# Block-diagonal score products of the first layer: one half of the heads for all four token tiles in a call, and the first softmax by half the heads of two tiles

## The reference, cut to what matters

```python
h = einsum('bnd,ade->bane', feat_in, W)
th = tanh(h)
attn = einsum('bane,aeo->bano', th, w_src) + swapaxes(einsum('bane,aeo->bano', th, w_dst), 2, 3)
attn = where(attn >= 0, attn, 0.2 * attn)
attn = softmax(where(~adj, -999.0, attn), axis=-1)
feat_out = einsum('banm,bame->bane', attn, h) + b
out = gate * elu(feat_out) + (1 - gate) * feat_in     # gate = sigmoid(feat_in @ H_w.T + H_b)
```

## Time and profile before

| | us |
|---|---|
| time, median of 3 runs | 1072.71 (1072.68 to 1074.22) |
| the profiled execution's own time | 1072.87 |
| its span from first to last instruction | 1070.8 |
| TensorE busy | 991.1 (93%) |
| VectorE busy | 780.3 (73%) |
| ScalarE busy | 574.5 (54%) |
| GpSimd busy | 277.7 (26%) |

### The profile page before, as it was taken

The page is one execution under the profiler, slowest core; times in us unless marked ns, Lnnn a source line. Parts: engine busy times, 40 slices in busy tenths (PEclk is TensorE's granted clock), DMA queues, the critical chain, the costliest instruction groups (busy, mean ns, idle before and its releaser), DMA issues.

```text
span 1070.8 us, 24885 instructions
## 1 busy us (share of the span) xinstructions
PE 991.1 (93%) x10153; PEld 857.0 (80%) x10153; DVE 780.3 (73%) x1456; ACT 574.5 (54%) x1126; POOL 277.7 (26%) x338
## 2 busy tenths in 40 slices
PE   6589999999999999999999999999999999999686
PEld 5487878888787887978788797878879788887575
DVE  4867867778786777868677886767788676876814
ACT  6556466373746636374564638446463754745331
POOL 2233140502415051240504124050321406032120
PEclk9689999999999999999999999999999999999988
DMA  9211151510414142031413204151241515111102
GB/s 237 32 15 20 29 90 32 90 32 31 61 32 91 31 82 40 31 62 32 91 32 77 41 12 83 31 91 31 65 39 19 91 32 90 32 47 18 28 30 59
DMA packets 183652, 56.41 MB, mean 53 GB/s; under 512 B 164978, under 2 KB 183540, under 8 KB 183540
## 3 DMA queue, kind: packets, MB, share of 16 engines
q1 hardware_dynamic: 183540, 54.83, 28.3%
HBM read 17.06 MB, written 12.58 MB: 28 GB/s over the span
## 4 chain that ended last, share of the span: by engine, by line
PE 55%; DVE 27%; ACT 7%; issue 7%; POOL 0%; ACTq 0%; DVEq 0%; POOLq 0%
PE ps L624 11%; PE ps L610 10%; PE ps L626 10%; PE ps L625 10%; DVE x L948 5%; PE ps L693 5%; PE ps L790 4%; DVE ee L945 4%; ACT p L430 3%; DVE hT1l L1056 3%; DVE hT0l L858 3%; DVE stats L842 3%; DVE p L973 2%; PE ps L808 2%; DVE x_in L996 2%
## 5 line engine op out<-in xcount | busy, mean ns | idle before, releaser
L410 POOL TENSOR_TENSOR x_in<-x_in,ee 128x384 f32<-128x384 f32 x64 | 72.5, 1134 | 626.7 <-DVE ee L951 626.7
L469 ACT ACTIVATE th<-ps 128x384 f32<-128x384 f32 x64 | 31.9, 499 | 209.8 <-DVE v_tok L936 209.8
L1020 DVE TENSOR_TENSOR hT1l<-ps,hT1h 128x512 fp32r<-128x512 f32 x48 | 30.4, 685 | 88.2 <-ACT hT1h L540 88.1
L984 DVE COPY_PREDICATED_SCALAR z<-not_adj,masked 128x768 f32 x64 | 69.4, 1084 | 32.5 <-ACT z L501 32.5
L610 PE MATMUL ps<-ident,p 128*128 128x128 f32 x576 | 76.3, 283 | 17.8 <-ACT p L430 10.0
L403 POOL TENSOR_TENSOR x_in<-x_in,h 128x384 f32<-128x384 f32 x64 | 85.5, 1367 | 18.5 <-DVE Wf_lo L883 18.5
L610 PEld LDWEIGHTS ps<-ident,p 128*128 128x128 f32 x576 | 65.3, 144 | 23.0 <-issue 12.7
L624 PE MATMUL ps<-Wf_hi,hT1h 128*128 128x384 f32 x192 | 69.0, 359 | 10.4 <-DVE hT1l L1056 10.4
L397 POOL TENSOR_TENSOR x_in<-x_in,bf_row 128x384 f32<-128x384 f32 x64 | 62.1, 1003 | 48.0 <-ACT p L430 48.0
L507 ACT ACTIVATE z<-z 128x768 f32<-128x768 f32 x64 | 54.5, 853 | 28.1 <-DVE z L989 28.0
L501 ACT ACTIVATE z<-ps 128x384 f32<-128x384 f32 x128 | 52.5, 497 | 31.0 <-PE ps L693 31.0
(11 more groups left out here) (130 smaller groups left out, 2796.5 us busy)
## 6 DMA issues: line engine op xcount, KB each, us to landing
V<-v_tok SPq DMA_DIRECT2D x128, 192.0 KB, 5.0
x_in<-in_x_dram SPq DMA_DIRECT2D x16, 768.0 KB, 5.0
out_dram<-x_in SPq DMA_DIRECT2D x16, 768.0 KB, 3.6
x<-in_L_gnn_H_w_dram SPq DMA_DIRECT2D x1, 576.0 KB, 5.9
QT<-in_L_gnn_W_dram SPq DMA_DIRECT2D x3, 192.0 KB, 6.7
thT<-in_L_gnn_Wq_dram SPq DMA_DIRECT2D x1, 576.0 KB, 5.8
z<-in_L_gnn_Wk_dram SPq DMA_DIRECT2D x1, 576.0 KB, 6.8
z<-in_L_gnn_Wv_dram SPq DMA_DIRECT2D x1, 576.0 KB, 7.9
```

The source lines that it names most:

```text
L410: pool.tensor_tensor(x_in[:, i % 3, t], x_in[:, i % 3, t], ee[:, t], ALU.subtract).then_inc(x2_made, 1)
L984: dve.copy_predicated(zt, not_adj[:, t].unsqueeze(1).broadcast_to((P, HEADS0, N)), masked0[:].unsqueeze(2).broadcast_to((P, HEADS0, N))).t ...
```

## The change

`blocks` and `leaky` go by halves of the heads instead of pairs of tiles. `blocks(half_of)` takes the banks of all four tiles for one half of the heads. Its eight calls run first over the four tiles of graph 0 of each tile and then over the four tiles of graph 1; the shapes, the number of calls, the operands and the place of both `blocks` in TensorE's program stay. `leaky` goes four times for half 0, then `copy_q(2)`, then four times for half 1. The bank of a job is now that of `4*half_of + t`.

`softmax0` and `exp0` go by a unit: unit 0 is half 0 of tiles 0 and 1, unit 1 half 0 of tiles 2 and 3, units 2 and 3 the same for half 1. A unit has as many elements as a tile had (768 in a partition), but as two runs of 384. `turn_probs` turns in the same order as before; it now waits for the unit in which a block lies, and asks at the middle of a tile as well: 12 waits in 24 turns where there were 8.

```diff
-                def blocks(pair):
-                    take(i, job("leaky_made", 4 * pair + 3))
-                    take(i, job("leaky_made", 4 * pair))
-                    take(i, job("leaky_made", 4 * pair + 1))
-                    take(i, job("leaky_made", 4 * pair + 2))
-                    for half_of in range(2):
-                        for t in (2 * pair, 2 * pair + 1):
+                def blocks(half_of):
+                    for t in range(TILES):
+                        take(i, job("leaky_made", 4 * half_of + t))
+                    for g in range(2):
+                        for t in range(TILES):
                             rows = slice(SD * t, SD * t + SD)
-                            for g in range(2):
-                                mm = pe.matmul(ps[64 * g:64 * g + 64, job("leaky_made", 2 * t + half_of) % BANKS, 0:D],
-                                               src_rows[rows, g * N:(g + 1) * N],
-                                               thT[rows].rearrange("p c m -> p (c m)")[:, (2 * g + half_of) * D:(2 * g + half_of + 1) * D],
-                                               start=True, stop=True, skip_group_check=True)
+                            mm = pe.matmul(ps[64 * g:64 * g + 64, job("leaky_made", 4 * half_of + t) % BANKS, 0:D],
+                                           src_rows[rows, g * N:(g + 1) * N],
+                                           thT[rows].rearrange("p c m -> p (c m)")[:, (2 * g + half_of) * D:(2 * g + half_of + 1) * D],
+                                           start=True, stop=True, skip_group_check=True)
                     mm.then_inc(scores0_full, 1)
...
+                def unit_of(t, pair):
+                    return 2 * (pair // PAIRS1) + t // 2 + 1
...
-                            if k == 0 or pair == 0:
-                                pe.wait_ge(ready, TILES * n + t + 1)
+                            if k == 0 or pair % PAIRS1 == 0:
+                                pe.wait_ge(ready, TILES * n + made(t, pair))
...
-                def softmax0(t):
+                def softmax0(unit):
                     if real(i):
-                        n = TILES * i + t + 1
-                        zt = z[:, t].rearrange("p (h m) -> p h m", m=N)
+                        n = TILES * i + unit + 1
+                        half_of, pair = divmod(unit, 2)
+                        tiles, heads = slice(2 * pair, 2 * pair + 2), slice(PAIRS0 * half_of, PAIRS0 * half_of + PAIRS0)
+                        zu = z[:, tiles, half_of * D:(half_of + 1) * D].rearrange("p t (h m) -> p t h m", m=N)
                         dve.wait_ge(not_adj_made, i + 1)
-                        dve.wait_ge(leaky_made, 8 * i + 2 * t + 2)
+                        dve.wait_ge(leaky_made, 8 * i + 4 * half_of + 2 * pair + 2)
```

More of the change, by code:

```diff
@@ L491, in copy_k, with leaky, exp0 @@
                                        bias=bk_col[:, c:c + 1]).then_inc(k_copied, 1)
-                def leaky(t):
+                def leaky(half_of, t):
                     if real(i):
[L495 to L499, removed]
-                        for half_of in range(2):
-                            act.activation(z[:, t, half_of * D:(half_of + 1) * D], ps[:, job("leaky_made", 2 * t + half_of) % BANKS, 0:D],
-                                           ACT.Prelu, alpha=SLOPE).then_inc(leaky_made, 1)
-                def exp0(t):
+                        if half_of == 0 and t == 0:
+                            if real(i - 1):
+                                act.wait_ge(probs0_turned, 6 * i)
+                            else:
+                                act.wait_ge(w_low, 3 * C)
+                        act.wait_ge(scores0_full, 2 * i + half_of + 1)
+                        act.activation(z[:, t, half_of * D:(half_of + 1) * D], ps[:, job("leaky_made", 4 * half_of + t) % BANKS, 0:D],
+                                       ACT.Prelu, alpha=SLOPE).then_inc(leaky_made, 1)
+                def exp0(unit):
                     if real(i):
-                        act.wait_ge(scores0_shifted, TILES * i + t + 1)
-                        act.activation(z[:, t], z[:, t], ACT.Exp).then_inc(probs0_made, 1)
+                        half_of, pair = divmod(unit, 2)
+                        zu = z[:, 2 * pair:2 * pair + 2, half_of * D:(half_of + 1) * D]
+                        act.wait_ge(scores0_shifted, TILES * i + unit + 1)
+                        act.activation(zu, zu, ACT.Exp).then_inc(probs0_made, 1)
                 def exp1(t):
@@ L551, in body @@
                 copy_q(1)
-                leaky(0)
-                leaky(1)
+                for t in range(TILES):
+                    leaky(0, t)
                 copy_q(2)
-                leaky(2)
-                leaky(3)
+                for t in range(TILES):
+                    leaky(1, t)
                 exp0(0)
@@ L767, in body, with tile_of, turn_probs @@
                     scores(1)
-                def turn_probs(name, ready, done, src, pairs, n, jobs):
+                def unit_of(t, pair):
+                    return 2 * (pair // PAIRS1) + t // 2 + 1
+                def tile_of(t, pair):
+                    return t + 1
+                def turn_probs(name, ready, made, done, src, pairs, n, jobs):
                     for q in range(jobs):
@@ L812, in body @@
                 if real(i):
-                    turn_probs("probs0T_copied", probs0_made, probs0_turned, z, PAIRS0, i, 6)
+                    turn_probs("probs0T_copied", probs0_made, unit_of, probs0_turned, z, PAIRS0, i, 6)
                 attend0(0)
@@ L816, in body @@
                 if real(j):
-                    turn_probs("probs1T_copied", probs1_made, probs1_turned, p1, PAIRS1, j, 3)
+                    turn_probs("probs1T_copied", probs1_made, tile_of, probs1_turned, p1, PAIRS1, j, 3)
                 attend0(2)
@@ L976, in shift1 @@
                                               ALU.subtract).then_inc(scores1_shifted, 1)
-                def softmax0(t):
+                def softmax0(unit):
                     if real(i):
-                        n = TILES * i + t + 1
-                        zt = z[:, t].rearrange("p (h m) -> p h m", m=N)
+                        n = TILES * i + unit + 1
+                        half_of, pair = divmod(unit, 2)
+                        tiles, heads = slice(2 * pair, 2 * pair + 2), slice(PAIRS0 * half_of, PAIRS0 * half_of + PAIRS0)
+                        zu = z[:, tiles, half_of * D:(half_of + 1) * D].rearrange("p t (h m) -> p t h m", m=N)
                         dve.wait_ge(not_adj_made, i + 1)
-                        dve.wait_ge(leaky_made, 8 * i + 2 * t + 2)
-                        dve.copy_predicated(zt, not_adj[:, t].unsqueeze(1).broadcast_to((P, HEADS0, N)),
-                                            masked0[:].unsqueeze(2).broadcast_to((P, HEADS0, N))).then_inc(masked, 1)
+                        dve.wait_ge(leaky_made, 8 * i + 4 * half_of + 2 * pair + 2)
+                        dve.copy_predicated(zu, not_adj[:, tiles].unsqueeze(2).broadcast_to((P, 2, PAIRS0, N)),
+                                            masked0[:].unsqueeze(2).unsqueeze(3).broadcast_to((P, 2, PAIRS0, N))).then_inc(masked, 1)
                         dve.wait_ge(masked, n)
-                        dve.tensor_reduce(mx0[:, t], zt, AX_X, ALU.max).then_inc(max0_made, 1)
+                        dve.tensor_reduce(mx0[:, tiles, heads], zu, AX_X, ALU.max).then_inc(max0_made, 1)
                         dve.wait_ge(max0_made, n)
-                        dve.tensor_tensor(zt, zt, mx0[:, t].unsqueeze(2).broadcast_to((P, HEADS0, N)), ALU.subtract)\
+                        dve.tensor_tensor(zu, zu, mx0[:, tiles, heads].unsqueeze(3).broadcast_to((P, 2, PAIRS0, N)), ALU.subtract)\
                             .then_inc(scores0_shifted, 1)
```

3 lines of the change are left out of this document (2 added, 1 removed).

## The result

The changed kernel takes 1054.42 us (median of 4 runs, 1053.49 to 1055.45) against 1073.06 us (1072.68 to 1074.22) before: the ratio is 0.9825, with a 95% interval of 0.9808 to 0.9842. It is 1.75% faster, 18.6 us by the medians. The forecast was 1053.5 us, in a range of 1050.5 to 1064.

The account below looks back on a forecast made before the run. TensorE's own queue was taken to set the pace from before the first `blocks` to the second-layer scores. 30 x 0.62 = 18.6 us plus 0.6 in iteration 0 made 19.2 us saved: 1053.5 us, range 1050.5 to 1064.

Parts of the forecast that it names:

- The path: From before the first `blocks` to the end of the second-layer scores, only TensorE's own queue sets the pace.
- Eight places: Each `blocks` on TensorE: two rounds of eight instead of four of four, 0.83 us in place of 1.45; chance 0.75.
- the rule of the Trainium skill: Weight loads overlap running multiplications only when row groups differ; `blocks` would keep four rounds, 1072.7 us.
- VectorE's cover: VectorE's idle time before `values1(0)` falls from 1.70 to 1.08 us, so VectorE does not become late.
- The forms at nothing: VectorE's softmax instructions as two runs of 384 with one dimension more cost nothing.
- The four waits more: Four more TensorE waits per iteration in the turns: taken as nothing, upper bound 0.6 us in all.
- The sum: Whole kernel: 18.6 us from iterations 1 to 15 plus 0.6 from iteration 0, together 19.2 us saved.
- three more turns at half clock: Iteration 0, TensorE behind the last exponential: nine turns left instead of six, a loss of 0.7 us.
- Four as the limit: Rival: TensorE runs only four at once, `blocks` stays 1.45 us, time 1072.7; chance 0.09.
- Three rounds: Rival: issue grouped by four calls, `blocks` takes three rounds, saving 0.32 us each, 1063 us; chance 0.05.
- Slower: Rival: a column half takes only two row groups at once, `blocks` 2.74 us, time 1111; chance 0.06.
- Eaten gain: Rival: gain partly lost to longer softmax instructions or a colder clock, 1056 to 1066 us; chance 0.05.

Follow-up runs that it names:

- same_half: Changed kernel with graph 1's calls writing graph 0's 64 PSUM partitions, so four places instead of eight: 1073.78 us, ratio to before 1.0005.
- graphs_inner: Changed kernel with the two loops of `blocks` exchanged, so neighbouring calls share a row group; same eight places: 1054.6 us, ratio to before 0.9828.
- units_only: Kernel before with only leaky, softmax, exponential and turns' waits by units of half the heads of two tiles: 1073.41 us, ratio 1.0002.
- halves_adjacent: Kernel before with `blocks` loops reordered so two calls on the same place follow each other; same four places: 1073.95 us, ratio 1.0001.

## Why the prediction was right, point by point

**The path.** That both `blocks` lie on a stretch where TensorE alone sets the pace held: the two save 2 x 0.62 = 1.24 us, and the iteration is 61.74 us where it was 62.98, in most of the steady ones. VectorE still waited for TensorE later on (1.00 us and 1.00 us).

**Eight places.** The step with the most risk, from rows that showed two and four places to eight, was right, with the 0.83 us as worked out. `same_half` shows that it is the places, and not the softmax, the banks or the order. That each place there is would be used was an extension of a pattern seen at two and four; no row here derived it, the prediction said so, and gave it 0.75. The row on which I rejected the rule of the Trainium skill, two of four calls at once in one row group, was the right one to look at: `graphs_inner` shows the same with eight calls.

**VectorE's cover.** Forecast 1.08 us before `values1(0)`, found 1.00. The first mask in iteration 0 was to come at 40.15 and came at 40.48, but the whole trace was 0.26 us later there (the first `blocks` at 37.75 instead of 37.49), a drift from before anything that was changed. The forms at nothing: `units_only` gives 1.0002.

**The four waits more.** Forecast nothing: the 24 turns take 2.84 us in the changed trace, as in the earlier trace rows.

**The sum.** 19.2 us were forecast, and 18.6 came by the medians. The two later comparisons, each on one chip, gave 19.4 (`graphs_inner`) and 19.1 (the changed kernel again), so the sum as a whole was met within what executions differ, some 2 us. By the spans of the two profiled executions it was 17.2, and about 1 us of the 2 missing is that the changed kernel's was the slowest of its four runs (1055.45 against a median of 1054.42). The terms, in the two traces: 14 steady intervals between first `blocks` gave 16.9 where 14 x 1.24 = 17.4 were due; iteration 0 gave 0.2 where 0.6 was; from the last first-`blocks` (at 969.86 and 952.99) to the end it was 0.3 where 1.24 was; 0.3 was lost before the first. The half us missing in the steady part is not the clock, which was 1.00 in all of these intervals. It goes with a stop of TensorE in the middle of line 813 (line 808 before), which the prediction did not have: 0.5, 0.7, 0.3 and 0.3 us in four intervals of the changed kernel, 0.4 and 0.4 us in two of the kernel before. One of them (engine, line, releaser: total, times, longest, in us):

```profile
PE ps L813 <- issue: 0.7, 1, 0.7
```

No row names what it waited for, and in the changed kernel's second profiled execution the 14 intervals came to 865.6 us, the full 17.5 less than before. So it is a difference between executions.

Outside the steady part I had allowed for the clock only in iteration 0, and with a wrong mechanism: I charged 0.7 us for three more turns at half clock behind the last exponential. They were no loss. The 21 turns took 54.71 - 50.39 = 4.32 us, the 18 before 55.78 - 51.43 = 4.35:

```profile
50.39 4.39 PE L612 MATMUL ps<-ident,z 128*128 128x128 f32 x21 [4.96 <-ACT z L509]
54.71 1.62 PE L795 MATMUL ps<-V,QT 128*64 128x66 f32 x48
```

TensorE's clock was back at 1.00 from 54 us on, where the kernel before had it from 57 on. TensorE was even 3.1 us ahead at 64 us, since a stretch at half clock that the kernel before had from 63.5 to 67 was missing. But then it had to wait for ScalarE's `th`, had half the clock, and ended 0.14 us behind. In the last iteration the 1.24 us were kept until the query products, of which more ran at half the clock: 18.1 us ahead at their start (1005.70 against 1023.81), 17.4 us at the turns that follow (1031.05 against 1048.48). Filling the idle stretches gave 1.6 to 3.0 us back. That the clock costs time at both ends is shown; that it accounts for each tenth is not. The forecast hit closely in part because a loss that was charged and did not come stood against losses that were not charged.

**The rivals.** Four as the limit: excluded, eight started within 0.07 us. Three rounds: excluded, there were two, and `halves_adjacent` shows that calls are not taken in groups of four. Slower: excluded, four row groups in one half took 1.45 us for eight calls, as the two by two places did before. Eaten gain: in part, in single executions, by the clock and not by VectorE.

## What to carry to other kernels

Small products should be listed by the place in the array that each takes, row group by column group, and calls between two waits should cover as many different places as there are; how they are ordered among themselves mattered little here (0.83 us in both orders over eight places, 1.45 and 1.47 over four). Such a regrouping changes which results are complete first, so the consumer has to be regrouped with it: here the products alone brought little more than half. When time is taken out of TensorE, look where it will now wait longer, and at the granted clock behind those waits, above all at the two ends of a program. And before a shortfall of 2 us is explained, look at how far executions of one kernel lie apart.

## What the runs showed of the hardware that I had not expected

A call whose place in the array was busy did not stop the calls behind it: with pairs of calls on the same place next to each other, four multiplications still started within 0.05 us, and eight calls took 1.47 us instead of 1.45, where strict order would have made it 3.4 by my estimate (five steps of 0.645 and 0.16).

The width was almost free: four calls on four row groups take 0.80 us and eight calls on eight places 0.83, in f32 with 384 columns.

After 2.01 us of idle time, one turn and 0.42 us more of idle time TensorE's granted clock went to 0.50, and twelve turns of 128x128 cost 2.36 us instead of 1.40. TensorE being earlier was what made the wait longer, so that 0.82 us of gain became a loss of 0.14. An idle stretch of 1.89 us, 15 us earlier, was followed by the full clock in that execution and by half the clock in others: the length of the wait alone did not decide it.
